# Local attention: weighted values of all four head pairs in one run, a round later

## The reference, cut to what matters

```python
h = shift_token(x)
q, k, v = split(h @ wqkv)                      # 256 -> 3 x 512
q = l2norm(q) * qs;  k = l2norm(k) * ksc
q, k = rotary_xpos(q, k)                       # q*cos + rotate_half(q)*sin, scaled
bk, bv = look_around(k), look_around(v)        # the window before and the window itself
sim = einsum('bhwid,bhwjd->bhwij', 8 * bq, bk) # 128 x 256
attn = softmax(where(mask, -max, sim))
out = einsum('bhwij,bhwjd->bhwid', attn, bv)   # the weighted values
x = x + out @ wo
```

## Time and profile before

| | |
|---|---|
| time before, median of 3 runs | 4484.74 us (4481.17 to 4498.85) |
| the profiled execution | 4477.03 us, its span 4475.2 us |
| granted TensorE clock, mean of the span | 0.973 |
| PE busy over the span | 4134.2 us, 92% |
| PEld busy | 2636.3 us, 59% |
| DVE busy | 3575.0 us, 80% |
| ACT busy | 2776.3 us, 62% |
| POOL busy | 1622.9 us, 36% |
| values of the local attention (L1531) | 3840 instructions, 268.0 us busy |
| weights turned (L1519) | 1920 instructions, 307.9 us busy |

### The profile page before, as it was taken

One profiled execution on the slowest core, in us unless ns is written; L12 is line 12 of the kernel. 1 busy time (PEld: TensorE's weight loads), 2 busy tenths in 40 slices (PEclk: granted clock), 3 DMA queues, 4 the chain that ended last, 5 costly groups with the idle time before them and its releaser, 6 DMA issues. The chain is left out here.

```text
span 4475.2 us, 79984 instructions
## 1 busy us (share of the span) xinstructions
PE 4134.2 (92%) x26906; PEld 2636.3 (59%) x26906; DVE 3575.0 (80%) x7980; ACT 2776.3 (62%) x6215; POOL 1622.9 (36%) x2440
## 2 busy tenths in 40 slices
PE   4959999999999996499999998999899999998998
PEld 2523333333333334377777776888777777777887
DVE  5669999999999976788888886556588888895665
ACT  1428888888888882067766665444567666664443
POOL 2400001000000002456655554454456555554555
PEclk8969999999999998799999999999999999999999
DMA  5952434434343315610000010212010000101321
GB/s 186 375 113 45 65 52 87 59 49 64 49 61 57 52 26 183 190 42 25 25 28 25 26 39 16 89 48 67 19 45 25 28 25 27 40 16 58 88 72 56
DMA packets 368445, 295.91 MB, mean 66 GB/s; under 512 B 66393, under 2 KB 325289, under 8 KB 368049
## 3 DMA queue, kind: packets, MB, share of 16 engines
q1 hardware_dynamic: 368048, 290.93, 26.5%
HBM read 178.56 MB, written 111.21 MB: 65 GB/s over the span
## 5 line engine op out<-in xcount | busy, mean ns | idle before, releaser
L896 ACT ACTIVATE fa_P<-fa_pS 128x512 f32<-128x512 f32 x2048 | 1111.7, 595 | 316.9 <-PE fa_pS L822 267.3
L923 DVE TENSOR_REDUCE fa_mx<-fa_pR 128x2 f32<-128x1024 f32 x1024 | 1205.7, 1221 | 92.8 <-PE fa_pR L803 78.2
L1683 POOL TENSOR_TENSOR wa_pn<-wa_pr,wa_ri 128x512 f32<-128x512 f32 (+1 forms) x512 | 673.2, 1316 | 493.8 <-DVE wa_ri L1735 493.6
L1621 ACT ACTIVATE wa_pr<-wa_sm,wa_mn 128x256 f32<-128x256 f32 (+1 forms) x1024 | 496.7, 488 | 177.7 <-DVE wa_mn L1726 151.4
L837 PE MATMUL fa_pO<-fa_P,fa_V 128*32 128x512 f32 x4096 | 546.5, 606 | 0.2 <-ACT fa_P L896 0.2
L822 PE MATMUL fa_pS<-fa_Q,fa_K 50*128 50x512 f32 x2048 | 508.1, 493 | 41.3 <-ACT fa_P L896 11.0
L822 PEld LDWEIGHTS fa_pS<-fa_Q,fa_K 50*128 50x128 f32 x2048 | 191.4, 184 | 517.2 <-ACT fa_P L896 431.4
L803 PE MATMUL fa_pR<-fa_K,fa_Q 48*128 48x512 f32 x2048 | 430.7, 464 | 57.2 <-DMA fa_K<-parts_d 38.3
L1150 POOL TENSOR_TENSOR ao_xn<-ao_xn,ao_mod 128x1024 f32<-128x1024 f32 x16 | 37.6, 2348 | 1092.1 <-DVE ao_xn L1115 1092.1
L1472 PE MATMUL wa_pQK<-wa_wqkv,wa_xT 128*128 128x512 f32 x1536 | 422.9, 412 | 6.3 <-DVE wa_qa L1772 6.3
L1726 DVE CUSTOM_DVE_ANT_0 wa_sm<-wa_pS,wa_mask 128x256 f32<-128x256 f32 (+1 forms) x1024 | 356.9, 402 | 19.0 <-issue 14.4
(11 more groups left out here) (185 smaller groups left out, 7104.5 us busy)
## 6 DMA issues: line engine op xcount, KB each, us to landing
parts_d<-pj_parts SPq DMA_DIRECT2D x64, 512.0 KB, 5.5
fa_Q<-parts_d SPq DMA_DIRECT2D x192, 128.0 KB, 4.3
fa_K<-parts_d SPq DMA_DIRECT2D x192, 128.0 KB, 7.5
v_d<-pj_v SPq DMA_DIRECT2D x16, 1024.0 KB, 8.5
fa_V<-v_d SPq DMA_DIRECT2D x32, 512.0 KB, 9.9
pj_x<-in_L_attn_x SPq DMA_DIRECT2D x16, 512.0 KB, 7.7
fa_Q<-fa_nrow SPq DMA_DIRECT2D x512, 2.0 KB
att_d<-fa_att SPq DMA_DIRECT2D x64, 128.0 KB, 2.5
```

What stands on the lines that cost most here:

```text
L896: nc.scalar.activation(Pr[:, k % 2, h, :], pS[:, (s * exped.per + u) % T, :], ACT.Exp).then_inc(exped.sem, 1)
L923: nc.vector.tensor_reduce(mx[:, q // QB, :, a, q % QB, kh], row_slot(), AX.X, ALU.max).then_inc(row_free, 1)
L1621: last = nc.scalar.activation(pr[:, hp % 2, hh, lo:], sm[:, hp % 2, hh, lo:], ACT.Exp, bias=mn[:, p, h:h + 1], scale=-1.0, accum_out=rs[:, ...
L1683: nc.gpsimd.tensor_tensor(pn[:, hp % 2, :, lo:], pr[:, hp % 2, :, lo:], inv, ALU.mult).then_inc(s["weighted"].sem, 1)
```

## The change

- PE: `values` no longer takes a group of pairs. It waits until all four pairs of the tile lie in pT, and issues the matmuls of all four in one run. It is called once for each tile, where the call for pairs 2 and 3 stood: in the round after the tile's attention, behind `scores` of pairs 0 and 1. The call behind `project` k goes. The semaphore `summed` counts one for each tile instead of two.
- pT gets four slots instead of two, one for each pair. ACT's `p_out` waits for `summed` of the tile before, where it waited for the values that last read its slot.
- DVE's last step of the rotation writes its sum over qb; qn goes, and PE turns qb. The wait for the transposition of the tile before (`k_turned`) moves from that step to the first one that writes qb, step 0.

```diff
-        p_turned=pairs, pT_ready=pairs, summed=2, o_high=1, o_ready=1,
+        p_turned=pairs, pT_ready=pairs, summed=1, o_high=1, o_ready=1,
...
-        qn = sb("qn", [P, 2, HEADS, DH])
...
-        pT = sb("pT", [P, 2, 2, 2, P])
+        pT = sb("pT", [P, PAIRS, 2, 2, P])
...
                         last = nc.tensor.transpose(dst[:, hp * P:(hp + 1) * P],
-                                                   qn[:, j, 2 * hp:2 * hp + 2, :].rearrange("p h c -> p (h c)"),
+                                                   qb[:, j, 2 * hp:2 * hp + 2, :].rearrange("p h c -> p (h c)"),
                                                    ident[:])
...
-                def values(n, w, grp):
-                    pe.wait_ge(s["pT_ready"].sem, s["pT_ready"].upto(g(n), 2 * grp + 2))
-                    if grp == 0 and not early(n, 1):
+                def values(n, w):
+                    pe.wait_ge(s["pT_ready"].sem, s["pT_ready"].upto(g(n)))
+                    if not early(n, 1):
                         pe.wait_ge(s["o_ready"].sem, s["o_ready"].upto(g(n - 1)))
-                    for hp in (2 * grp, 2 * grp + 1):
+                    for hp in range(PAIRS):
...
-                                                        pT[:, hp % 2, hh, side, :], start=(side == sides(w)[0]),
+                                                        pT[:, hp, hh, side, :], start=(side == sides(w)[0]),
...
                     if within(end):
-                        values(end, w_end, 1)
+                        values(end, w_end)
...
                     if within(att):
-                        values(att, w_att, 0)
                         turn_p(att, w_att, 2)
...
-                    if not fresh(n, hp):
-                        act.wait_ge(s["summed"].sem, g(n) * 2 + hp // 2)
+                    if not early(n, 1):
+                        act.wait_ge(s["summed"].sem, s["summed"].upto(g(n - 1)))
                     side = sides(w)[0]
-                    nc.scalar.copy(pT[:, hp % 2, :, side:2].rearrange("p h w t -> p h (w t)"),
+                    nc.scalar.copy(pT[:, hp, :, side:2].rearrange("p h w t -> p h (w t)"),
...
                         dve.wait_ge(s["scaled"].sem, s["scaled"].upto(g(n)))
+                        if step == 0 and not early(n, 1):
+                            dve.wait_ge(s["k_turned"].sem, s["k_turned"].upto(g(n - 1)))
...
                         dve.wait_ge(c.sem, c.upto(g(n), 3))
-                        if not early(n, 1):
-                            dve.wait_ge(s["k_turned"].sem, s["k_turned"].upto(g(n - 1)))
-                        ins = nc.vector.tensor_tensor(qn[:], qa[:], qb[:], ALU.add)
+                        ins = nc.vector.tensor_tensor(qb[:], qa[:], qb[:], ALU.add)
```

## The result

The changed kernel takes 4570.07 us (median of 4 runs, 4562.65 to 4576.83) against 4487.76 us for the kernel before: 1.0181 times as long, with a 95% interval of 1.0157 to 1.0204. That is 82 us more where 81 were forecast. The profiled execution has a span of 4560.9 us, 85.7 more than before.

The account below looks back on a forecast made before the run. PE and the DVE chain were taken to bound the full round at once. Longer rounds add 40.5 us per attention stage, 81 for two, to the 4484.7 us median: 4566 us, range 4535 to 4605.

Parts of the forecast that it names:

- Two bounds at once: Full round: PE and the DVE chain both bind; turn of q has 0.27 us of slack, turn of pair 3 none.
- PE's gain of 0.17 per tile: Values on PE: one merged group saves a 1.03 us slot and costs 0.86, for PE alone 0.17 us gained.
- The delay at the entry, 0.86: Values end 0.86 us later; ACT's o_out and DVE's split_o, with all queued behind them, start that much later.
- The slack of 0.11 at the end of the round: From turn of x to next scores: 0.33 us needed, 0.44 seen, so a full round grows 0.75 us to 14.35.
- The rounds around window 0: The round attending to window 0 (half the keys) was to grow 0.86 us, the round after it 0.32.
- Rounds with a weight piece: Rounds splitting a piece of feed-forward weights: full ones +0.2 us to 14.35, the two other kinds +0.5 and +0.2.
- Add in place, moved wait, four slots: DVE's sum over qb, its wait at the first half-rotation, pT's four slots: 0 us; the add's bounds 0 and +0.75 per round.
- The sum of the rounds: Rounds 3 to 63 of an attention stage: 31.5 + 5.2 + 2.2 + 1.6, 40.5 us per stage, 81 for two.
- The mis-sized term: Last three rounds of each attention stage: taken as 0, with 1.5 us either way per stage.
- PE as the bound: Rival, chance 0.12: PE sets the round, only its saving of 0.17 us is left, 21 us less, 4464 us.
- The rival of the in-place add: Rival, chance 0.04: DVE's sum over its input costs +0.75 us a round on top, some 96 more, 4660 us.
- the clock rival: Rival, chance 0.03: the clock falls in PE's new gaps, about 1 us more of chain in 122 rounds, 4690 us.

Follow-up runs that it names:

- the first experiment: Kernel before with all parts of the change but the merge, the values staying in two calls at their old places: 4489.95 us, ratio 1.0002.
- the tail experiment: Changed kernel, but each stage's last two tiles keep their values in two calls at the old places: 4569.76 us, ratio 1.0173 to the kernel before.
- the last one: Changed kernel with exponentials 0, 1, inverses 0, 2, 3 and scale moved earlier, and the last two tiles' values in two calls: 4479.86 us, ratio 0.9975.
- scale first, no merge: Kernel before with DVE's order alone altered, scale of mid ahead of split_o and inverse 0: 4518.75 us, ratio 1.0073.

## Why the prediction was right, point by point

- *Two bounds at once* held. The turn of q and the turn of pair 3 both moved, and the latter set the round: the turn of pair 3 at +13.52 (predicted +13.53), released by POOL, the turn of q at +12.32 (+12.33). The copy of k ends at +14.09 (+14.11), 0.23 ahead of the next scores (0.09 before), so that branch no longer binds.
- *PE's gain of 0.17 per tile*: measured 2.05 - 1.90 = 0.15. It was not seen in any time, as said.
- *The delay at the entry, 0.86*: 0.88 at the copy, 0.87 at the end of the sum. Nothing absorbed it on the way.
- *The slack of 0.11 at the end of the round*: 0.93 us from the turn of pair 3 to the next scores before, 0.80 after, so 0.13. Full round +0.71 for +0.75.
- *The rounds around window 0* were the weaker terms: the one that attends to it went from 11.73 to 12.47, +0.74 for +0.86; the next from 13.17 to 13.58, +0.41 for +0.32. The two errors nearly cancel.
- *Rounds with a weight piece*: the full ones 14.32, as forecast (14.35): the piece is hidden by the later start. The one that attends to window 0 went from 12.05 to 12.52 (+0.47 for +0.5), the one behind it from 13.87 to 14.41, +0.54 where +0.2 was forecast.
- *Add in place, moved wait, four slots*: 0 as taken, shown by the first experiment.
- *The sum of the rounds*: 38.0 and 38.1 us measured for 40.5 each. The measured sums end with the last turn of x; the forecast has one round more (0.75), which lies in the tail's stretch and gained 0.44 there up to the next scores.
- **The mis-sized term** is the last rounds: 0 with 1.5 either way, measured +2.8 and +7.2 us (47.0 to 49.8, 44.4 to 51.6). I had looked at the one tail of the first stage, where a group ran at half speed anyway, and took the second for its like; its granted clock had been 1.00 and is 0.83 now. The rounds' excess of 5 us and the tails' lack of 10 let the total come out close. That the total was met this closely was partly luck; the full round's 0.71 for 0.75 was not. The tails are those of one execution of each kernel, and, as shown above, what they have to do with the merge is open.
- *The rivals.* PE as the bound fell: PE was busy 13.57 of 13.60 us, and delaying what ACT and DVE wait for made the round longer one for one once 0.13 to 0.17 us of slack were used. The Trainium skill's advice cited with this rival ("Perfetto Trace Analysis", Identifying the Most-Contended Engine) would have had 4464 us; the measurement, 4570, decides against taking PE's busy time for the bound here; the same section warns that matmul busy time is a poor measure of how near PE is to its limit. The rival of the in-place add fell with the first experiment. In the full rounds the granted clock stayed at 1.00; the clock rival was right only in the tail, where nothing in the sum had a price for it.

## What to carry to other kernels

A merge that saves work on the busiest engine can still lose if its result is what other engines' queues stand behind: look at which instruction waits for the result, and at all that is queued after it on its engine, before counting the saving. Here, where the order of every engine is written by hand, the same merge made a full round 0.71 us longer, left it as it was, or made it 0.41 shorter, by the order around it, so move the waiting instruction back in its queue together with the change. And an engine that shows 13.57 of 13.60 us busy need not be the only one that sets the pace; a round of the same work that takes longer, somewhere in the same trace, tells.

## What was not expected of the hardware

- The stretches before the first attention stage, which no kernel here touches, took 1888.6 us in the profiled execution of the changed kernel and 1902.0 in that of the tail experiment; the jump lies between 1528 us and the start of the attention's output stage (1707.7 and 1722.6). Between 1640 and 1700 us the granted clock is 1.00 in the one and 0.78 in the other, in the same part of the program; why was not followed up. The runs of one kernel lie in groups: 4563 to 4564 and 4576 to 4577 for the changed kernel; 4467 to 4468, 4480 and 4486 to 4489 for the last one. It is a reason to compare by stage and not by span where the difference is small.
- The granted clock in the last three rounds of a stage, in which PE idles 0.7 to 2.4 us at a time, was anything from 0.83 to 1.00 for nearly the same work; between the two stages of one kernel (scale first, no merge) 0.85 for 1.00 came with 4.7 us more.
